# A gated cross-attention block on one core: the order of TensorE's first tiles, the first loads, and who computes the low parts of the weights

## The reference: what is computed

```python
x = x + tanh(g_xattn[0]) * attention(layernorm(x), ctx, ctx)    # 16 heads, causal, softmax
z = layernorm(x)
idx  = top_k(softmax(z @ w_router + b_router), 4)                # 4 of 16 blocks
mask = one where a block is in idx
h = relu(einsum('nd,ebd->neb', z, w1b) + b1b)
y = einsum('neb,ebd,ne->nd', h, w2b, mask) + b2
x = x + tanh(g_ffn[0]) * y
```

## Time and profile before

| | |
|---|---|
| three executions, us | 763.47, 763.25, 758.12 |
| profiled execution, us | 759.15 |
| its span on the core, us | 757.4 |
| mean granted clock of TensorE | 0.991 |
| TensorE matmuls busy | 726.0 us, 96% of the span |
| VectorE busy | 532.1 us, 70% |
| GpSimd busy | 488.3 us, 64% |
| ScalarE busy | 442.0 us, 58% |
| TensorE's share of the chain that ended last | 92% |

### The profile page before, as it was taken

How to read it: one execution, slowest core, us unless ns; L and a number is a source line. 1 busy time by engine, 2 the same in 40 slices (tenths; PEclk the granted TensorE clock), 3 DMA queues, 4 the chain that set the end, 5 groups by cost and what they waited for, 6 DMA issues and landing times.

```text
span 757.4 us, 31152 instructions
## 1 busy us (share of the span) xinstructions
PE 726.0 (96%) x13576; PEld 675.0 (89%) x13576; DVE 532.1 (70%) x1428; ACT 442.0 (58%) x812; POOL 488.3 (64%) x663
## 2 busy tenths in 40 slices
PE   4769999999999999999999999999999999999888
PEld 3658999999999999999999999999999999999787
DVE  5468776776777687677677677767767767766552
ACT  3467566556556656655655655665665565565442
POOL 6587676666667667667666666766766766665542
PEclk9699999999999999999999999999999999999999
DMA  4212101111110111110111111011111011000000
GB/s 148 86 33 58 31 18 45 44 47 31 45 43 19 44 46 32 45 45 19 43 46 44 32 45 45 18 45 45 35 40 45 21 42 45 18 3 16 16 24 33
DMA packets 32182, 29.93 MB, mean 40 GB/s; under 512 B 6064, under 2 KB 31792, under 8 KB 32048
## 3 DMA queue, kind: packets, MB, share of 16 engines
q1 hardware_dynamic: 31776, 26.90, 11.6%
q10 hardware_dynamic: 272, 1.05, 0.4%
HBM read 19.03 MB, written 8.39 MB: 36 GB/s over the span
## 4 chain that ended last, share of the span: by engine, by line
PE 92%; ACT 3%; DVE 2%; DMA 1%; issue 1%; SPq 0%; POOLq 0%; POOL 0%; ACTq 0%
PE score_banks L300 10%; PE score_banks L273 8%; PE bank L414 8%; PE bank L313 8%; PE bank L393 8%; PE bank L416 8%; PE bank L415 8%; PE bank L395 7%; PE bank L394 7%; PE bank L240 5%; PE bank L251 4%; PE bank L330 3%; PE bank L341 3%; ACT weights L469 1%; PE score_banks L283 1%; PE bank L354 1%
## 5 line engine op out<-in xcount | busy, mean ns | idle before, releaser
L714 POOL TENSOR_SCALAR_AFFINE_SELECT weights<-weights 128x1024 f32<-128x1024 f32 x128 | 137.7, 1100 | 133.4 <-ACT weights L469 133.3
L721 POOL TENSOR_TENSOR h_low<-hid,h_high 128x512 fp32r<-128x512 f32 x128 | 165.9, 1297 | 28.0 <-ACT hid L491 25.1
L619 DVE SCALAR_TENSOR_TENSOR hid<-bank,b_cols,used_all 128x256 f32<-128x256 f32 x248 | 108.0, 477 | 69.8 <-PE bank L395 64.4
L393 PE MATMUL bank<-xT_high,w_high 128*128 128x256 f32 x496 | 149.6, 302 | 0.0
L469 ACT ACTIVATE weights<-score_banks 128x1024 f32<-128x1024 f32 x128 | 124.2, 1023 | 38.7 <-PE score_banks L300 38.7
L414 PE MATMUL bank<-w_high,h_high 128*128 128x256 f32 x488 | 140.6, 288 | 4.0 <-DVE y_out L604 3.3
L395 PE MATMUL bank<-xT_high,w_low 128*128 128x256 f32 x496 | 139.4, 281 | 0.0
L394 PE MATMUL bank<-xT_low,w_high 128*128 128x256 f32 x496 | 139.3, 281 | 0.0
L416 PE MATMUL bank<-w_high,h_low 128*128 128x256 f32 x488 | 137.9, 283 | 0.0
L415 PE MATMUL bank<-w_low,h_high 128*128 128x256 f32 x488 | 137.8, 282 | 0.0
L414 PEld LDWEIGHTS bank<-w_high,h_high 128*128 128x128 f32 x488 | 92.2, 189 | 6.6 <-DVE y_out L604 4.1
(11 more groups left out here) (92 smaller groups left out, 1450.9 us busy)
## 6 DMA issues: line engine op xcount, KB each, us to landing
c_in<-in_ctx SPq DMA_DIRECT2D x32, 256.0 KB, 2.9
x_in<-in_x SPq DMA_DIRECT2D x32, 256.0 KB, 3.2
out_y<-y_out SPq DMA_DIRECT2D x31, 256.0 KB, 2.2
qT<-qT SPq DMA_DIRECT2D x128, 4.0 KB
w_stage<-in_w1T ACTq DMA_DIRECT2D x1, 1024.0 KB, 5.8
hid<-in_w2T SPq DMA_DIRECT2D x8, 128.0 KB, 2.7
out_y<-y_out SPq DMA_DIRECT2D x2, 128.0 KB, 1.7
b_all<-in_b SPq DMA_DIRECT2D x1, 128.0 KB, 5.5
```

Of the source, the lines that this page charges most:

```text
L393: pe.matmul(out=bank, lhsT=w1_high[:, k, c], rhs=high, start=k == 0, stop=False)
L619: dve.scalar_tensor_tensor(hid[:, n % 4, j], hid_bank(n)[:, j * TOKS:(j + 1) * TOKS], b1_cols[:, c:c + 1], used_all[:, p % 2], ALU.add, AL ...
L714: pool.affine_select(out=w, in_=w, compare_op=ALU.is_ge, fill=0.0, base=0, pattern=[[0, 2 * HB], [1, S]], channel_multiplier=-1).then_inc( ...
L721: pool.tensor_tensor(h_low[:, p % 2, chunks], hid[:, n % 4], h_high[:, p % 2, chunks].bitcast(F32), ALU.subtract).then_inc(h_low_made, 1)
```

## The change

Seven edits, all of which act before the feed-forward part begins:

1. In iterations up to 4 TensorE turns the queries of tile i+2 ahead of `scores(i+1)` instead of behind; in iterations -2 and -1 the keys too.
2. Before the loop TensorE does 24 turns of the identity matrix into a bank that nothing reads (`WARM`).
3. Tile 0 of x is loaded by a DMA of its own with its own semaphore, then tile 1, then tiles 2 and 3; the first two loads of the context go out from ScalarE's queue instead of SyncE's.
4. ScalarE takes one exponential of a scratch column at the start, ahead of its wait for x.
5. The pieces of the weights are made in iterations 0 to 3 (before: -1, 0, 2, 3). Of the two pieces of an iteration GpSimd computes the low part of the first and VectorE that of the second, at the end of its iteration.
6. VectorE makes the mask tiles before the loop instead of in iteration -3, and GpSimd the small matrices they are cut from.
7. `q_pad` and `v_pad` are zeroed only in their upper 16 of 32 columns per head.

```diff
         def pieces_of(i):
-            n = {-1: 0, 0: 2, 2: 4, 3: 6}.get(i, 8)
-            return range(n, n + 2) if n < 8 else ()
+            return range(2 * i, 2 * i + 2) if 0 <= i < 4 else ()
...
             pe.wait_ge(ident_made, 1)
+            for n in range(WARM):
+                pe.transpose(banks[HID_BANK][:, 0:P], ident[:], ident[:])
             for i in ITERATIONS:
...
+                first = i < FFN_LAG
+                if first and 0 <= i + 2 < N:
+                    q_transposed(i + 2)
+                if i < 0 <= i + 2:
+                    k_transposed(i + 2)
                 if 0 <= i + 1 < N:
                     scores(i + 1)
-                if 0 <= i + 2 < N + MAX_LAG:
+                if not first and i + 2 < N + MAX_LAG:
                     q_transposed(i + 2)
-                if 0 <= i + 2 < N:
+                if i >= 0 and i + 2 < N:
                     k_transposed(i + 2)
...
+            for n in range(2):
+                tiles = slice(n * PAIR, (n + 1) * PAIR)
+                act.dma_start(c_in[:, tiles, :], A_ctx[tiles].rearrange("b p d -> p b d")).then_inc(c_landed[n], 16)
+
+            act.wait_ge(numbers_set, 2)
+            act.activation(scratch[:], half_power[:], ACT.Exp)
             act.wait_ge(x_landed[1], 16)
...
+            def weights_low(i):
+                for n in pieces_of(i)[1:]:
+                    _w, stage, high, low = w_piece(n)
+                    dve.wait_ge(w_high_made, n + 1)
+                    dve.tensor_tensor(low, stage, high.bitcast(F32), ALU.subtract).then_inc(w_low_also_made, 1)
...
-            dve.memset(q_pad[:], 0.0).then_inc(q_zeroed, 1)
+            dve.memset(q_pad[:, :, :, HD:], 0.0).then_inc(q_zeroed, 1)
...
                 if p is not None:
                     hidden_masked(p, m + 1)
+                weights_low(i)
                 if i == 1:
...
             def weights_low(i):
-                for n in pieces_of(i):
+                for n in pieces_of(i)[:1]:
                     _w, stage, high, low = w_piece(n)
                     pool.wait_ge(w_high_made, n + 1)
                     pool.tensor_tensor(low, stage, high.bitcast(F32), ALU.subtract).then_inc(w_low_made, 1)
...
-            load(0)
-            load(1)
+            sync.dma_start(x_in[:, 0, :], A_x[0]).then_inc(x_first_landed, 16)
+            sync.dma_start(x_in[:, 1:PAIR, :], A_x[1:PAIR].rearrange("b p d -> p b d")).then_inc(x_landed[0], 16)
+            sync.dma_start(x_in[:, PAIR:2 * PAIR, :], A_x[PAIR:2 * PAIR].rearrange("b p d -> p b d")).then_inc(x_landed[1], 16)
```

More of the change, by code:

```diff
@@ L30 @@
 FFN_LAG = 5
+WARM = 24
 OUT_LAG = 7
@@ L78, in build @@
         minus_one = sb("minus_one", [P, 1], F32)
+        scratch = sb("scratch", [P, 1], F32)
         gates = sb("gates", [P, 2], F32)
@@ L135, in build @@
         y_out = sb("y_out", [P, 2, 2, D], F32)
+        x_first_landed = sem("x_first_landed")
         x_landed = [sem(f"x_landed{i}") for i in range(XS // PAIR)]
@@ L166, in build @@
             "top_found", "clipped_made", "clipped_found", "marked_made"))
+        w_low_also_made = sem("w_low_also_made")
         gated_b2_made, adding_made = sem("gated_b2_made"), sem("adding_made")
@@ L380, in hidden @@
                 if m == 0 and p == 0:
-                    pe.wait_ge(w_low_made, 4)
+                    pe.wait_ge(w_low_made, 2)
+                    pe.wait_ge(w_low_also_made, 2)
                 n = PIECES * p + m
@@ L407, in ffn_out @@
                 if half == 0 and b == 0:
-                    pe.wait_ge(w_low_made, 8)
+                    pe.wait_ge(w_low_made, 4)
+                    pe.wait_ge(w_low_also_made, 4)
                 if t == 0:
@@ L550, in layernorm_stats @@
                 n, slot = divmod(landed(b), XS // PAIR)
-                dve.wait_ge(x_landed[slot], 16 * (n + 1))
+                if b == 0:
+                    dve.wait_ge(x_first_landed, 16)
+                else:
+                    dve.wait_ge(x_landed[slot], 16 * (n + 1))
                 stats_of(x_in[:, b % XS, :], stats1, mv1, b % 2, b, x_stats, x_mean)
@@ L611, in hidden_masked @@
                     dve.wait_ge(b1_landed, 16 * HC)
-                    dve.wait_ge(w_low_made, 8)
+                    dve.wait_ge(w_low_made, 4)
+                    dve.wait_ge(w_low_also_made, 4)
                 if m == 0:
@@ L651, in _ @@
             dve.memset(place[:], 0.0).then_inc(place_zeroed, 1)
+            dve.wait_ge(place_zeroed, 1)
+            dve.wait_ge(ident16_made, 1)
+            dve.wait_ge(triangle_made, 1)
+            for u in range(U):
+                rows = slice(u * PAD, (u + 1) * PAD)
+                dve.tensor_copy(place[rows].rearrange("p (j w) -> p j w", j=U)[:, :, 0:PAD],
+                                ident16[rows, rows].unsqueeze(1).to_broadcast([PAD, U, PAD])).then_inc(mask_made, 1)
+                dve.tensor_copy(tri[rows], triangle[rows, rows].unsqueeze(1).to_broadcast([PAD, HB, PAD])
+                                ).then_inc(mask_made, 1)
             dve.wait_ge(q_levels_set, LEVELS)
@@ L671, in _ @@
                     normalised(i + 3)
[L672 to L681, removed]
                 if 0 <= i - 3 < N:
@@ L733, in _ @@
                                base=0, pattern=[[-1, P]], channel_multiplier=1).then_inc(ident_made, 1)
-            pool.memset(v_pad[:], 0.0).then_inc(v_zeroed, 1)
+            pool.memset(ident16[:], 0.0).then_inc(ident16_zeroed, 1)
+            pool.memset(triangle[:], 0.0).then_inc(triangle_zeroed, 1)
+            pool.wait_ge(ident16_zeroed, 1)
+            pool.affine_select(out=ident16[:], in_=ident16[:], compare_op=ALU.not_equal, fill=1.0,
+                               base=0, pattern=[[-1, P]], channel_multiplier=1).then_inc(ident16_made, 1)
+            pool.wait_ge(triangle_zeroed, 1)
+            pool.affine_select(out=triangle[:], in_=triangle[:], compare_op=ALU.is_ge, fill=NEG, base=0,
+                               pattern=[[-1, P]], channel_multiplier=1).then_inc(triangle_made, 1)
+            pool.memset(v_pad[:, :, :, HD:], 0.0).then_inc(v_zeroed, 1)
             pool.wait_ge(v_zeroed, 1)
@@ L760, in _ @@
                     hidden_low(p, m + 1)
[L761 to L769, removed]
                 weights_low(i)
```

## The result

| | median, us | executions, us |
|---|---|---|
| before | 762.46 | 763.47, 763.25, 758.12, 761.67 |
| changed | 771.40 | 771.72, 773.42, 770.73, 771.09 |

The ratio is 1.0133 with a 95% interval of 1.0088 to 1.0177; it is formed from all executions, and the two medians alone give 1.0117. The forecast was 769 with a range of 761 to 777: right in sign and roughly in size (+9.7 us forecast, +8.9 between the medians, +12.5 between the two profiled spans). Its likeliest class, within 1% with 54%, was not the one that came; the measured 771.4 lies 0.5 above the 770.9 from which it counted as slower by over 1%.

A forecast was written before the change was run, and what follows sets the result against it. The way of the maxima was taken to bound the first tiles, before TensorE fills at iteration 5. Head -4.0, wait +9.5 and clock +4.2 make +9.7 on 759.15: 769 us, range 761 to 777.

The forecast's parts named there:

- likeliest class: Whole kernel: a difference below 1%, 7.6 us, from the kernel before; 54%, against 38% slower and 8% faster.
- The wait: Iterations 2 to 4: query turns, now ahead of scores, wait for VectorE's weight subtraction and product; +9.5 us (+6.5 to +10.2).
- VectorE beside GpSimd: Weight subtractions: VectorE's waits for GpSimd's and ends 3.4 us after the exponentials, 2.3 if unhindered.
- The clock: TensorE after the new gaps: turn, scores and key turn of three tiles run at 1.2 GHz; +4.2 us, floor 0, ceiling +9.6.
- The head: Start to the end of tile 1's exponentials: earlier turns, higher clock and reordered loads gain; -4.0 us (-6.0 to -0.6).
- E0: End of tile 0's exponentials: 22.37 us before, forecast near 19.4, or 22.8 if the clock is low.
- E1: End of tile 1's exponentials: 32.97 us before, forecast 29.0.
- Behind E4: From the end of tile 4's exponentials to the kernel's end: 699.6 us, kept unchanged.
- E4: End of tile 4's exponentials, just before iteration 5: 57.79 us before, forecast near 67.
- The chances: Whole kernel against the kernel before: 8% faster by over 1%, 54% within 1%, 38% slower by over 1%.

The follow-up runs named there:

- e1: Changed kernel with GpSimd computing the low part of all eight weight pieces and VectorE none: 757.50 us, ratio 0.9969 to the kernel before.
- e3: Changed kernel with VectorE's weight subtraction moved behind the next iteration's row maximum: 753.97 us, ratio 0.9938 to the kernel before; again 755.30 us, 0.9937.
- e6: Kernel before with only VectorE's share of the weights added, pieces in the old iterations: 766.94 us, ratio 1.0083 to the kernel before.
- e4: Changed kernel with 40 unread turns of the identity ahead of the query turns in iterations 2, 3 and 4: 766.67 us, ratio 1.0091 to the kernel before.
- e9: Changed kernel with GpSimd's own weight subtraction put one iteration later, behind its second reciprocal root: 769.73 us, ratio 1.0118 to the kernel before.
- e8: e3 with 20 unread identity turns ahead of tile 2's turns and 10 ahead of tile 3's: 751.45 us, ratio 0.9895 to the kernel before.
- e7: Kernel before with only the changed order of turns on TensorE, weights as before: 759.09 us, ratio 0.9985 to the kernel before.
- e5: Changed kernel without the 24 identity turns at the start: 774.36 us, ratio 1.0183 to the kernel before.
- e10: e8 with VectorE's normalisation of tile 2 put ahead of the first row maximum: 751.59 us, ratio 0.9897 to the kernel before.

## Why the prediction was right, and where its sizes were off

**The wait** was right in mechanism (e1, e3, e6) and size: +9.5 forecast, +8.7 at full clock (e4). The turns began 4.0, 3.9 and 3.9 us after the exponentials, forecast 4.2.

**VectorE beside GpSimd.** The forecast let VectorE's subtraction end 0.7 after GpSimd's. Measured 0.55 after, and e9 shows that the duration is GpSimd's doing: 0.69 alone, 1.48 beside it. The rule of the Trainium skill (SBUF — State Buffer, "SBUF: two separate sides"), by which whichever of the two starts first has the shared ports for its whole instruction, agrees so far: VectorE's operation stood in its slot until GpSimd's was over. In iteration 1 it was the one-input `gated_b` that waited, 1.35 instead of 0.34, while the subtraction ahead of it, begun first at 32.27, took 0.79 and GpSimd's begun at 32.48 took 1.70. The row that I had put beside the rule, 0.81 against 0.41, was of a one-input operation too, while my sentence on the rule spoke of two inputs; the subtraction, which has two, bears it out.

**The clock** was undersized: +4.2 forecast, +6.1 measured. The 0.8 by which the wait was oversized hides part of that, which is luck: the tiles came out at +14.8 against +13.7. I had charged turn, scores and key turn at 1.2 GHz. The chain shows the attention product too at 1.89 to 1.94 instead of 1.08 in iterations 2 and 3; the level rose only behind it. Twice the difference, 1.7, makes most of the 1.9 that was missing.

**The head** is the step that failed most: -4.0 forecast, -1.8 measured. E0 was 22.42 instead of 19.4. Three things were missing. The rows are from the timeline of the changed kernel:

```profile
4.68 0.18 DVE L690 COPY tri<-triangle 32x128 bf16<-32x128 bf16 x1
4.90 0.43 DVE L566 BATCH_NORM_STATS2 stats<-x_in 128x6 f32<-128x256 f32 x1
...
12.21 0.68 DVE L590 TENSOR_REDUCE q_pad<-score_banks 128x8 f32<-128x512 f32 x1
...
13.36 0.38 DVE L581 TENSOR_SCALAR q_pad<-x_in,mv,rstd 128x256 f32<-128x256 f32 x1
...
13.79 0.42 PEld L244 LDWEIGHTS bank<-ident,q_pad 128*128 128x128 f32 x4 [2.91 <-DVE q_pad L581]
```

and one window of 1 us (columns as in the earlier trace rows):

```profile
14.00:15.00 1.00, 1.00 (x31) 0.82 (x35) 0.00 (x0) 0.50 (x1) 0.82 (x2) 0.66 0.00 0
```

First, the forecast let the mask copies go ahead of the first statistics for nothing. Tile 0's own load was issued at 0.79 and landed 2.6 us later, at 3.4, but VectorE was at the mask copies until 4.86, so the statistics began at 4.90, later than the 4.55 of before; the first turns began at 7.18 instead of 6.6 and scores(0) at 9.77 instead of 9.1. Second, the turns of tile 2 at 13.79 wait for its normalised queries, which VectorE makes behind both maxima and one more set of statistics; I had let them go at 12.35, with the maxima, which were done at 12.89. Third, the level I had kept high until E0 fell at 14.3, in the second scores: they took 1.64 and the shifted scores 2.12 instead of 1.22. TensorE had idled from 11.1 to 13.8. Together 0.7 + 0.9 + 0.6 + 0.9 = 3.1 us, all that E0 was late by. E0 to E1, on the other hand, was 8.8 and not 9.6, since the clock rose at 28. For the clock e8 is the test: with that gap and the next filled, E0 is 20.7, 1.1 to 1.3 less than in e3's two profiles and 1.7 less than here.

Edits 3, 4, 6 and 7 were not undone one by one. What the profiles show of the head is this: the order of turns alone put E0 at 25.38 (e7), all edits but the 24 turns at 24.75 (e5), all of them at 22.42. So the order cost 3.0 up to E0, the 24 turns gave 2.3 back, and the rest together about as much as two profiles can differ by. Up to E0 the head won nothing against the 22.37 of before; its -1.8 lies between E0 and E1, 8.8 instead of 10.6, half of it in the shifted scores, 1.15 instead of 2.07.

**Behind E4** little changed, 699.0 against 699.6, as assumed.

**The chances.** I gave 54% to within 1% and 38% to slower. The centre was 2.8 us of span low, 2.2 of it in the head; E4 came at 70.9 and not near 67. The median of before that I set it against stands in a spread of 5 us. Whether that spread is the clock's is not shown for the kernel before, of which one execution was profiled.

## What to carry to other kernels

Before giving a helper engine part of a preparation, look at what it does next in its own fixed order and who waits for that; the same four subtractions cost about 15 us more in one slot than in another (ratios 1.0133 and 0.9938, of 760 us). When a turn or load is moved ahead of other work on an in-order engine, its waits move ahead too. Price an idle gap on TensorE twice, for the gap and for the pieces that run at half the clock behind it; where the gap is known, turns that nothing reads can hold the clock (e8: 3.9 us faster than e3 taken beside it), if they end before the wait does; in e10 they did not.

## What the runs showed of the hardware

With 10 to 40 turns of a 128 x 128 tile put into a gap, the granted clock stayed at 1.00 (2.4 GHz) through gaps of up to 5 us in every profile that had them: e4 from 30 us on, where 40 took 4.53 us, and e8 and e10 throughout, where 20 took 2.40. (The 24 turns at the start took 5.38 in e8 and 4.38 in e10, against 2.9 at the rate of those 20, so the level rose only while they ran, though the row reads 1.00.) Without them it fell to 0.50 at 34.8 in the changed kernel, in the first gap that e4 fills, and at 14.3, behind the one that e8 fills. A VectorE operation that met GpSimd's subtraction grew by 0.79 (subtraction) and 1.01 us (one-input scaling); GpSimd's subtraction grew from 1.27 to 1.70 where VectorE's had begun first. The clock level of the first tiles can make two executions of one kernel differ by 3 us: e3's two profiled ones, 750.9 and 753.9 us of span, differ between E0 and E4, and the second had the low level from 24 to 34 us. With the clock at 1.00 in all six, e8's executions spread over 1 us; e10's, three of them at a mean of 0.998, over 2.4 (750.84 to 753.23). The kernel before spreads from 757.2 to 763.5. That this too is the clock's is likely and not shown; its mean granted clock cannot settle it, because of the first low stretch that the clock's row leaves out.
